# Cross attention and a mixture of experts: one reduction less, other instruction orders in the prologue and in chunk 0, weight splits moved from GpSimd to VectorE

## The reference

```python
x = x + attend(layernorm(x) @ Wq + bq, ctx @ Wk + bk, ctx @ Wv + bv, mask)   # softmax over 154 keys
t = layernorm(x)
scores = sigmoid(l2norm(t) @ l2norm(gate_w).T)         # 16 experts
topk_w = top_k(scores, 8), divided by its sum
y = silu(t @ w_gate[e]) * (t @ w_up[e]) @ w_down[e]    # every e
x = x + sum_e(y * combine) + shared(t)
```

## Time and profile before

| | us |
|---|---|
| median of 3 runs | 650.99 (650.79 to 651.32) |
| the profiled execution | 650.85 |
| its span, first to last instruction | 648.7 |
| TensorE busy | 634.6 (98%) |
| VectorE busy | 472.7 (73%) |
| GpSimd busy | 294.7 (45%) |
| ScalarE busy | 235.7 (36%) |
| mean granted TensorE clock | 0.997 |

### The profile page before, as it was taken

One profiled execution on the slowest core, in us unless ns is written; L12 is line 12 of the kernel. 1 busy time (PEld: TensorE's weight loads), 2 busy tenths in 40 slices (PEclk: granted clock), 3 DMA queues, 4 the chain that ended last, 5 costly groups with the idle time before them and its releaser, 6 DMA issues.

```text
span 648.7 us, 10466 instructions
## 1 busy us (share of the span) xinstructions
PE 634.6 (98%) x3688; PEld 551.5 (85%) x3688; DVE 472.7 (73%) x941; ACT 235.7 (36%) x500; POOL 294.7 (45%) x275
## 2 busy tenths in 40 slices
PE   8898999999999999999999999999999999999997
PEld 7576888889888888888888898888888888888886
DVE  3779897868967588766868689675887768575443
ACT  5644444333243323433243332433234332432221
POOL 2517687333743356333563337433464334423333
PEclk9999899999999999999999999999999999999999
DMA  7265663424225324053244342263240531242100
GB/s 212 68 168 193 175 176 79 149 70 151 63 35 198 90 83 97 24 174 107 74 89 131 89 148 64 36 198 98 73 98 22 177 107 42 56 132 98 65 1 33
DMA packets 112655, 67.19 MB, mean 104 GB/s; under 512 B 80996, under 2 KB 102396, under 8 KB 112604
## 3 DMA queue, kind: packets, MB, share of 16 engines
q1 hardware_dynamic: 111516, 65.74, 36.0%
q10 hardware_dynamic: 1088, 0.79, 0.4%
HBM read 55.79 MB, written 10.42 MB: 102 GB/s over the span
## 4 chain that ended last, share of the span: by engine, by line
PE 91%; DVE 5%; issue 2%; ACT 1%; POOL 1%; POOLq 0%; ACTq 0%; DVEq 0%
PE y_ps L393 9%; PE gate_ps L395 9%; PE gate_ps L394 9%; PE up_ps L395 9%; PE up_ps L394 9%; PE gate_ps L393 9%; PE up_ps L393 9%; PE y_ps L394 9%; PE y_ps L395 9%; PE f_ps L538 2%; DVE hs L1155 1%; DVE W L999 1%; PE up_ps L402 1%; PE f_ps L575 1%; PE f_ps L393 1%
## 5 line engine op out<-in xcount | busy, mean ns | idle before, releaser
L1351 POOL TENSOR_TENSOR hidden<-hidden,cb 128x512 f32<-128x512 f32 x128 | 193.9, 1515 | 278.5 <-DVE hidden L1149 234.3
L866 ACT ACTIVATE hidden<-gate_ps 128x512 f32<-128x512 f32 x136 | 81.3, 598 | 292.9 <-PE gate_ps L395 292.9
L1145 DVE SCALAR_TENSOR_TENSOR hidden<-hidden,gate_ps 128x512 f32<-128x512 f32 x136 | 92.7, 681 | 102.9 <-ACT hidden L866 102.7
L393 PE MATMUL y_ps<-W,hs 128*128 128x256 f32 x544 | 154.7, 284 | 5.0 <-DVE hs L1155 5.0
L394 PE MATMUL y_ps<-W,hs 128*128 128x256 f32 x544 | 151.6, 279 | 0.0
L395 PE MATMUL y_ps<-W,hs 128*128 128x256 f32 x544 | 151.4, 278 | 0.0
L1155 DVE TENSOR_TENSOR hs<-hidden,hs 128x512 fp32r<-128x512 f32 x136 | 111.1, 817 | 21.8 <-ACT hs L873 21.6
L393 PEld LDWEIGHTS y_ps<-W,hs 128*128 128x128 f32 x544 | 102.2, 188 | 13.6 <-ACT hs L873 5.0
L393 PE MATMUL gate_ps<-xT,W 128*128 128x512 f32 x272 | 107.9, 397 | 0.0
L395 PE MATMUL gate_ps<-xT,W 128*128 128x512 f32 x272 | 107.6, 396 | 0.0
L394 PE MATMUL gate_ps<-xT,W 128*128 128x512 f32 x272 | 107.3, 395 | 0.0
(11 more groups left out here) (162 smaller groups left out, 664.0 us busy)
## 6 DMA issues: line engine op xcount, KB each, us to landing
cb<-c_rows SPq DMA_DIRECT2D x64, 512.0 KB, 4.8
blocks<-in_x_dram SPq DMA_DIRECT2D x28, 128.0 KB, 2.9
xin<-in_x_dram SPq DMA_DIRECT2D x7, 512.0 KB, 4.1
t_rows<-blocks SPq DMA_DIRECT2D x28, 128.0 KB, 2.7
xs<-t_rows SPq DMA_DIRECT2D x7, 512.0 KB, 3.5
out_dram<-x SPq DMA_DIRECT2D x7, 512.0 KB, 6.2
p_rows<-blocks SPq DMA_DIRECT2D x28, 80.0 KB, 2.3
stage<-in_L_ffn_w_gate_dram SPq DMA_DIRECT2D x16, 128.0 KB, 2.5
```

The source lines that it names most:

```text
L393: mm(ps, lh, rh, start=first and i == 0, stop=False)
L866: af(ew[:, i, :], gate_ps[:, i, :], ACT.Tanh, scale=0.5).then_inc(tanh_done, 1)
L1145: V_.scalar_tensor_tensor(out=ew[:, i, :], in0=ew[:, i, :], scalar=1.0, in1=gate_ps[:, i, :], op0=ALU.add, op1=ALU.mult).then_inc(silu_don ...
L1351: pg.tensor_tensor(h[:, i, :], ew[:, i, :], cb[:, pair % PLACES, (e - 1) % 2, :], ALU.mult) \
```

## The change

The negated maximum is made by the reduction itself, and the multiplication and its semaphore go. `POOL_SPLITS` shrinks to experts 0 and 1, so that VectorE makes the low parts of experts 6, 8, 10, 12, 14 and 16 too. Several calls stand elsewhere in their engine's order: in the tables `exps`, `swap_p` and `add_bias`; in the prologue the split of the V tails (now in a first part for batch 0 and a second for the others), `turn_router`, `router_scaled`, `ln2`, `split_hi(3)`; in chunk 0's loop `hidden_hi` is ahead of `split_hi` and `hidden_lo` ahead of `split_lo` and of the front; in the last chunk, gate and up of expert 16 are ahead of down 13.

```diff
-ACT_AT = dict(exps=(1.5, 2), ...
-DVE_AT = dict(maxes=(.5, 1.5), swap_p=(2.5,), ...
+ACT_AT = dict(exps=(1.5, 2.5), ...
+DVE_AT = dict(maxes=(.5, 1.5), swap_p=(3,), ...
-POOL_SOON = dict(add_bias=(9.5,), ...
+POOL_SOON = dict(add_bias=(12.5,), ...
-        POOL_SPLITS = (0, 1, 6, 8, 10, 12, 14, 16)
+        POOL_SPLITS = (0, 1)
             def move_v_tails():
-                sp.wait_ge(vt_split, 4)
+                sp.wait_ge(vt_split, 2)
@@ tensor, prologue (and the same wait in values(1))
             attend(0, 0)
-            turn_router()
             attend(0, 1)
             values(1, y_ps[:, 0, 0:D])
+            turn_router()
@@ tensor, loop
                 for s in range(NE):
+                    if not ahead and s + AHEAD == NE - 1:
+                        gate(c, NE - 1)
+                        up(c, NE - 1)
                     down(c, s)
                     if ahead:
                         front(s, c + 1)
-                    if (s + AHEAD < NE or ahead) and not (c == 0 and s == 1):
+                    if (s + AHEAD < NE - 1 or ahead) and not (c == 0 and s == 1):
@@ scalar
-            def write_vt_hi():
+            def vt_hi_first():
                 act.wait_ge(vt_made, 1)
                 act.wait_ge(v_made, 1)
                 for row in (0, PAD):
                     ins = af(Vtail[row:row + PAD, 0, :], y_ps[0:PAD, 0, D:2 * D], ACT.Copy)
-                ins.then_inc(vt_split, 1)
+                ins.then_inc(vt0_split, 1)
+
+            def write_vt_hi():
+                act.wait_ge(v_lo, 1)
                 af(vt[:, HI, :], y_ps[:, 0, D:2 * D], ACT.Copy).then_inc(vt_split, 1)
@@ scalar, prologue
             exps(0, 0)
-            write_vt_hi()
+            exps(0, 1)
+            vt_hi_first()
             write_v_hi(0, y_ps[:, 0, 0:D])
-            exps(0, 1)
             probs_hi_first(0)
             probs_hi_first(1)
+            write_vt_hi()
...
             router_hi()
-            split_hi(3)
             t2_hi_first(0)
             t2_hi_first(1)
+            split_hi(3)
@@ scalar, loop
+                    if s + 1 < NE or ahead:
+                        hidden_hi(c, s + 1)
                     if c == 0 and s + EARLY < NE:
                         split_hi(s + EARLY)
-                    if s + 1 < NE or ahead:
-                        hidden_hi(c, s + 1)
@@ vector, mask_and_max
-                V_.tensor_reduce(rsum[:, 2 * q:2 * q + 2], att[:, 2 * q:2 * q + 2, 0:KEYS], AX_X, ALU.max) \
-                    .then_inc(maxes, 1)
-                dve.wait_ge(maxes, upto(c, 2, q + 1))
-                V_.tensor_scalar(nmax[:, 2 * q:2 * q + 2], rsum[:, 2 * q:2 * q + 2], -1.0, None, ALU.mult) \
+                V_.tensor_reduce(nmax[:, 2 * q:2 * q + 2], att[:, 2 * q:2 * q + 2, 0:KEYS], AX_X, ALU.max, negate=True) \
                     .then_inc(maxed, 1)
@@ vector, prologue
-            router_scaled()
-            write_vt_lo()
+            vt_lo_first()
             write_v_lo(0, y_ps[:, 0, 0:D])
             sum_reciprocal(0)
             probs_lo_first(0)
             probs_lo_first(1)
+            write_vt_lo()
+            router_scaled()
             residual(0, 0)
             ln2(0, 0)
             residual(0, 1)
+            ln2(0, 1)
             ln2_scale(0, 0)
-            ln2(0, 1)
             ln2_scale(0, 1)
@@ vector, loop
+                    if c == 0 and s + EARLY < NE:
+                        hidden_lo(c, s + 1)
+                        if s + EARLY not in POOL_SPLITS:
+                            split_lo(s + EARLY)
                     if ahead:
                         front(s, c + 1)
                     if c + 2 < CHUNKS:
                         soon(s, c + 2)
-                    if c == 0 and s + EARLY < NE and s + EARLY not in POOL_SPLITS:
-                        split_lo(s + EARLY)
-                    if s + 1 < NE or ahead:
+                    if (c > 0 or s + EARLY >= NE) and (s + 1 < NE or ahead):
                         hidden_lo(c, s + 1)
@@ gpsimd, add_bias
-                pool.wait_ge(maxes, upto(c - 1, 2, 2))
+                pool.wait_ge(scaled, upto(c - 1, 2, 2))
```

More of the change, by code:

```diff
@@ L22 @@
 PE_AT = dict(scores=(0, .5), attend=(5.5, 6), logits=(12,), turn_z=(12.5,), turn_c=(14.5,))
-ACT_AT = dict(exps=(1.5, 2), probs_hi=(5,), t2_hi=(11.5,), read_z=(12.5,), tanh_scores=(13,), combine_rows=(15,))
-DVE_AT = dict(maxes=(.5, 1.5), swap_p=(2.5,), sum_reciprocal=(3.5,), probs_lo=(5,), residual=(6, 6.5),
+ACT_AT = dict(exps=(1.5, 2.5), probs_hi=(5,), t2_hi=(11.5,), read_z=(12.5,), tanh_scores=(13,), combine_rows=(15,))
+DVE_AT = dict(maxes=(.5, 1.5), swap_p=(3,), sum_reciprocal=(3.5,), probs_lo=(5,), residual=(6, 6.5),
               ln2=(6.5, 7), ln2_scale=(8, 8.5), swap_x2=(8.5,), t2_lo=(11.5,), sum_logits=(13,), top_eight=(13.5,),
@@ L29 @@
 DVE_SOON = dict(ln1=(10, 10.5), swap_x=(15.5,))
-POOL_SOON = dict(add_bias=(9.5,), ln1_std=(11.5, 11.5), add_bv=(13.5, 14.5))
+POOL_SOON = dict(add_bias=(12.5,), ln1_std=(11.5, 11.5), add_bv=(13.5, 14.5))
 POOL_FIRST = dict(ln1_std=(.5, .5), add_bv=(2.5, 4.5))
@@ L166, in xattn_moe_kernel @@
         (consts_set, tail_zeroed, ctx_turned, ctxT_read, wq_turned, wq_summed, wq_mean, wqT_read, kt_made, kt_read, a_made, a_read,
-         bq_spread, brow_made, brow_scaled, v_made, v_hi, v_lo, vt_made, vt_split, vt_loaded, gate_summed, gate_inv, gate_scaled,
+         bq_spread, brow_made, brow_scaled, v_made, v_hi, v_lo, vt_made, vt0_split, vt_split, vt_loaded, gate_summed, gate_inv, gate_scaled,
          gate_turned, gate_split, keep_set, pads_set, bias_first, w_hi, w_lo_dve, w_lo_pool) = (
@@ L170, in xattn_moe_kernel @@
                              "kt_read", "a_made", "a_read", "bq_spread", "brow_made", "brow_scaled", "v_made",
-                             "v_hi", "v_lo", "vt_made", "vt_split", "vt_loaded", "gate_summed", "gate_inv", "gate_scaled", "gate_turned",
+                             "v_hi", "v_lo", "vt_made", "vt0_split", "vt_split", "vt_loaded", "gate_summed", "gate_inv", "gate_scaled", "gate_turned",
                              "gate_split", "keep_set", "pads_set", "bias_first", "w_hi", "w_lo_dve", "w_lo_pool"))
-        (ln1_stats, ln1_rstd, x_swapped, p_swapped, x2_swapped, t1_turned, t1_read, bias_added, x_biased, scored, scaled, maxes, maxed, exped,
+        (ln1_stats, ln1_rstd, x_swapped, p_swapped, x2_swapped, t1_turned, t1_read, bias_added, x_biased, scored, scaled, maxed, exped,
          rsummed, p_turned, p_hi, p_lo, attended, x2_made, ln2_stats, ln2_rstd, inv_norms, ln2_done, t2_turned, t2_hi,
@@ L178, in xattn_moe_kernel @@
             sem(n) for n in ("ln1_stats", "ln1_rstd", "x_swapped", "p_swapped", "x2_swapped", "t1_turned", "t1_read", "bias_added", "x_biased", "scored",
-                             "scaled", "maxes", "maxed", "exped", "rsummed", "p_turned", "p_hi", "p_lo", "attended",
+                             "scaled", "maxed", "exped", "rsummed", "p_turned", "p_hi", "p_lo", "attended",
                              "x2_made", "ln2_stats", "ln2_rstd", "inv_norms", "ln2_done", "t2_turned", "t2_hi",
@@ L489, in values @@
                     pe.wait_ge(v_lo, 1)
-                    pe.wait_ge(vt_split, 4)
+                    pe.wait_ge(vt_split, 2)
                 elif b == 2:
@@ L971, in mean_wq, with vt_lo_first, write_vt_lo @@
                 V_.tensor_scalar(wq_sum[:, KD:2 * KD], wq_sum[:, 0:KD], -1.0 / D, None, ALU.mult).then_inc(wq_mean, 1)
-            def write_vt_lo():
-                dve.wait_ge(vt_split, 2)
+            def vt_lo_first():
+                dve.wait_ge(vt0_split, 1)
                 dve.wait_ge(v_hi, 1)
                 V_.tensor_tensor(Vtail[2 * PAD:STACK, 0, :], y_ps[0:PAD, 0, D:2 * D], Vtail[0:PAD, 0, :].bitcast(F32),
-                                 ALU.subtract).then_inc(vt_split, 1)
+                                 ALU.subtract).then_inc(vt0_split, 1)
+            def write_vt_lo():
+                dve.wait_ge(vt_split, 1)
                 V_.tensor_tensor(vt[:, LO, :], y_ps[:, 0, D:2 * D], vt[:, HI, :].bitcast(F32), ALU.subtract) \
```

1 line of the change is left out of this document (removed).

## The result

The changed kernel takes 667.39 us (median of 6 runs, 663.97 to 669.23) against 650.89 (6 runs) of the kernel before in the same comparison: a ratio of 1.0245, 95% interval 1.0211 to 1.0279. The profiled execution took 668.61 us with a span of 666.5, 17.8 more than the span of before.

A forecast was written before the change was run, and what follows sets the result against it. TensorE, busy 634.6 of 648.7 us, bounds the kernel, so each new wait is paid in full. 650.85 - 0.9 + 10.0 + 1.0 + 4.7 - 1.1 = 664.5, given as 664; range 653 to 669.

The forecast's parts named there:

- slow clock: After the 7 us wait in chunk 0 the granted clock may fall again: +1.0 us, between 0 and 1.7.
- prologue, to turn_z: Earlier exps and ln2, partly taken back by V-tail transfers delaying expert loads: -0.9 us, bounds -2.7 and +0.3.
- rest of chunk 0, to logits(1): VectorE's row with six more splits and late swap_p makes logits(1) start at 116.8, not 106.76: +10.0 us, bounds +3, +13.
- chunks 2 to 7: swap_p behind silu_up(5) makes P land later, so each attend waits 0.3 to 1.3 us: +4.7 us, bounds 0 and +8.6.
- the end: Last chunk: gate and up of expert 16 before down 13 remove the 0.92 wait before down 16: -1.1 us, bounds -1.2, 0.
- swap_p(1) and the first attend: Chunk 0: swap_p at 67.65, P landing at 77.1, attend(1,0) at 82.8 before-time, a TensorE wait of 7.2 us.
- Splits: Chunk 0: splits on VectorE wait for GpSimd's weighting and should take 1.7 to 2.2 us, not 0.95.
- the collision: VectorE operations with two SBUF inputs and GpSimd operations lock each other out for whole instructions: 1.79 against 0.68 us.
- Costed at nothing: Edits given no time: add_bias at 12.5, exps(1) behind hidden_hi(3), turn_router, vt in two steps; negated reduction taken at 0.47 us.

The follow-up runs named there:

- e1_act_first: The changed kernel with hidden_hi and split_hi ahead of the front on ScalarE too in chunk 0: 665.95 us, ratio 1.0223.
- a1_tables: The changed kernel with the table entries of exps and swap_p back at 2 and 2.5: 659.50 us, ratio 1.011.
- a2_loop: The changed kernel with chunk 0's old loop order on ScalarE and VectorE (hidden_hi behind split_hi, hidden_lo behind front and split_lo): 659.03 us, ratio 1.0104.
- b1_swap: The kernel before with only the table entries exps at (1.5, 2.5) and swap_p at 3: 658.94 us, ratio 1.0098.
- a3_splits: The changed kernel with experts 6, 8, 10, 12, 14 and 16 split by GpSimd again: 663.37 us, ratio 1.0166.
- c1_read_z: The kernel before with the negated maximum, new prologue and last chunk's order, but ScalarE's split_hi(3) and split_hi(4) behind read_z(0): 648.00 us, ratio 0.9941.
- b3_neg_tail: The kernel before with only the negated maximum and the last chunk's new order: 647.70 us, ratio 0.9948.
- e3_bias: c1_read_z with add_bias at 12.5: 645.89 us, ratio 0.9917.
- b2_splits: The kernel before with only the six splits moved from GpSimd to VectorE: 654.58 us, ratio 1.0041.

## Why the prediction was right, point by point

**Direction and size.** 664 was forecast, 667.39 measured, inside 653 to 669. The profiled span moved by 17.8, where the sum said 13.7. By its terms, with the slow clock that TensorE paid for taken out of the stretches it fell in:

| term | forecast | measured |
|---|---|---|
| prologue, to turn_z | -0.9 | -0.3 |
| rest of chunk 0, to logits(1), without slow clock | +10.0 | +9.4 |
| slow clock (1.6 behind turn_z, 2.7 behind attend(1,0)) | +1.0 | +4.3 |
| chunks 2 to 7 | +4.7 | +4.1 |
| the end | -1.1 | -1.0 |
| the last store | none | +1.3 |
| sum | +13.7 | +17.8 |

**swap_p(1) and the first attend.** Predicted, with the 0.9 won in the prologue taken off: P lands at 76.2, TensorE is ready at 74.7, attend starts at 81.9, a wait of 7.2. Measured: 77.48, 76.13, 83.12 and 6.99. All three came 1.2 to 1.4 us later, so the wait is nearly as forecast. From the landing to the attend I had 5.7, measured 5.64. The wait has two causes, and each was taken away alone: without the queue behind the landing it is 4.50 (e1_act_first, 5.64 down to 3.39), with swap_p early it is 3.83 (a1_tables). Without either it is 0.48 (a2_loop). That swap_p comes late is itself the work of two edits: with the late table and the old order it starts at 64.04 (b1_swap) and 63.76 (a2_loop), with the early table and the new order at 63.01 (a1_tables), and only with both at 68.16.

**Rest of chunk 0.** +10.0 was forecast to logits(1). By the table of stretches it is -2.2 + 6.6 + 7.7 = +12.1, of which 2.7 are slow clock. The prediction doesn't give the late waits (1.94, 1.11, 2.73) one by one, only the end of VectorE's row; the runs show that the one at down 10 comes with the order alone, and those at down 12 and logits(1) in full only with order and splits together.

**Splits.** A split on VectorE takes 2.03 us in the median in this order, as the collision has it; the prediction had 1.7 to 2.2. What I did not see is that in the order of before it would stay at 0.95, with hidden_lo dearer instead. The Trainium skill's rule (SBUF — State Buffer, "SBUF: two separate sides") that the two engines lock each other out for whole instructions agrees again with a3_splits' L1089, 2.17 us against 0.68, and with c1_read_z's L1162, 1.90 against 0.69.

**Chunks 2 to 7.** +4.7 was forecast. From attend of chunk 2 to that of chunk 7 it is +3.7 and 0.4 before it: 4.1. The waits in the rows are 0.41, 0.36, 0.35, 0.44, 0.90 and 0.47, 2.9 together; I had 0.7, 1.3, 0.85, 1.1, 0.5 and 0.3. The other 1.2 us is that each stop costs about 0.2 us beside its wait: the period from 168.29 to 244.62 is 76.33, that of before 75.80, 0.53 longer with a wait of 0.36. So the direction and the mechanism are right, and that the sum is so close is luck: the waits were put too high, and the cost of a stop was not in it. a1_tables and b1_swap show from both sides that the table entries make these waits.

**The clock: the step that was mis-sized.** The prediction gave +1.0, "between 0 and the 1.7 of before"; 4.3 us were paid, most of what is missing between forecast and measurement. About the 7 us wait it is down from 78 to 90 us, with 2.7 us lost behind 83.12, and after the 1.9 us wait at turn_z it is down a first time, for 1.6 us, which I did not expect at all. This second part is partly chance: a1_tables, a3_splits and e1_act_first have it behind waits of 2.08 to 2.28 (10.45 to 10.52 us from turn_z to down(0,0)), a2_loop has not.

**Prologue.** -0.9 was forecast. turn_z came 0.34 earlier, not 0.85 (the V-tail transfers began at 23.25, not 22.5; ScalarE read the logits at 34.76). Its wait of 1.92 was there. The slow clock behind it turned the gain into a loss of 1.3 at down(0,0). c1_read_z confirms that ScalarE's weight splits held turn_z.

**The end.** -1.1 was forecast and the add on VectorE came 1.03 earlier against the last attend. The final store then took 5.2 us to the span's end instead of 3.9. No term stood for it, and it follows no edit that I can name: it is 4.0 in b3_neg_tail and c1_read_z and 6.1 in e3_bias.

**Costed at nothing.** The negated reduction costs no more than the plain one: its median over 16 is 474 ns, as that of L1067 before. add_bias at 12.5 was not nothing but a small gain in e3_bias; in the changed kernel it was not tested alone.

## What to carry to other kernels

When a transfer lies between two halves of a front, count every queue that it crosses at its new place, and look at what stands *behind its landing* on each: there a late landing is paid in the sum of all that waits in order. Where operations of two engines hold each other up, as those of VectorE and GpSimd did here, look at what each will be doing at the same moment; which of two operations waits is decided by the order, and only the one that TensorE needs matters. And a wait of TensorE costs more than its length where the clock falls after it, so give that a range and not a point. The parts that won here (the sign in the reduction with the last gate and up ahead of a down, which were measured together; read_z ahead of the splits; add_bias later) took waits away.

## What the runs showed that I had not expected

- The same wait of TensorE is followed by the lower clock in one trace and not in another. Behind a wait of 1.9 to 2.3 us at turn_z it fell in four traces and stayed at 1.00 in a2_loop (wait 2.01); in b2_splits down 2 waits 2.56 us and the clock is 1.00 in every window to 635 us; behind 1.06 us at 74 us it fell in c1_read_z and not in e3_bias. So a difference of 1 to 2 us between two single profiles can be the clock alone.
- The runs of the changed kernel scatter by 0.8% (663.97 to 669.23, mean clock 0.988 to 0.994, the two shortest with the highest clock). Those of b3_neg_tail, with a mean clock of 0.999 to 1.000, agree within 0.1% but for one (650.58, at 1.000), so not all scatter is the clock.
- Each stop of TensorE in the steady part costs about 0.2 us on top of its wait.
- The last store's time to the end of the span varies from 3.9 to 6.1 us between kernels whose last store is the same.
